# A transformer layer on one core: the next batch's input transposed in 64-row halves

## The reference

```python
x = L0_attn_x                                   # (8, 512, 256)
x = x + attn(layernorm(x), gamma, w_qkv, w_out)
x = x + ffn(layernorm(x), router_w, w1, b1, w2, b2)

# attn: xn = x / max(norm(x), 1e-12) * 16 * (gamma + 1)
#       q, k, v = split(xn @ w_qkv)             # 16 heads of 64
#       out = softmax(q * 64**-0.5 @ k.T) @ v @ w_out
# ffn:  p = top-2 of softmax(x @ router_w), divided by its sum
#       out = (gelu(x @ w1 + b1) @ w2 + b2) * sum(p)
```

## Time and profile before

| | |
|---|---|
| median of 3 runs | 1197.71 us (1197.66 to 1198.62) |
| profiled execution | 1198.14 us, its span 1196.3 us |
| TensorE busy | 1183.7 us (99%) |
| VectorE busy | 961.9 us (80%) |
| ScalarE busy | 884.3 us (74%) |
| GpSimd busy | 640.1 us (54%) |
| eight transpositions of an input (L610) | 1.04 us |

### The profile page before, as it was taken

How to read it: one execution, slowest core, us unless ns; L and a number is a source line. 1 busy time by engine, 2 the same in 40 slices (tenths; PEclk the granted TensorE clock), 3 DMA queues, 4 the chain that set the end, 5 groups by cost and what they waited for, 6 DMA issues and landing times. The chain is left out here.

```text
span 1196.3 us, 29198 instructions
## 1 busy us (share of the span) xinstructions
PE 1183.7 (99%) x11347; PEld 1040.4 (87%) x11347; DVE 961.9 (80%) x1714; ACT 884.3 (74%) x1914; POOL 640.1 (54%) x809
## 2 busy tenths in 40 slices
PE   8999999999999999999999999999999999999999
PEld 6778888888888888888888888888888888988988
DVE  7788789878988888888888888889888987666644
ACT  6888788888887888788888887888888884334432
POOL 5776556555655565556555655555555674222221
PEclk9999999999999999999999999999999999999999
DMA  4222111311121113111311131113111232121100
GB/s 132 66 77 66 34 40 30 95 25 35 36 88 35 37 37 89 37 37 37 89 37 36 37 89 37 36 37 89 37 37 37 72 86 79 36 69 39 36 19 36
DMA packets 35240, 62.91 MB, mean 53 GB/s; under 512 B 5920, under 2 KB 12576, under 8 KB 35104
## 3 DMA queue, kind: packets, MB, share of 16 engines
q1 hardware_dynamic: 35104, 61.05, 19.0%
HBM read 19.08 MB, written 8.39 MB: 23 GB/s over the span
## 5 line engine op out<-in xcount | busy, mean ns | idle before, releaser
L927 POOL TENSOR_SCALAR prob<-prob,rowinv 128x512 f32<-128x512 f32 x512 | 350.2, 699 | 290.6 <-DVE rowinv L1116 290.2
L836 ACT ACTIVATE prob<-ps,negmax 128x512 f32<-128x512 f32 x512 | 347.0, 686 | 34.1 <-DVE negmax L1111 29.7
L1035 DVE TENSOR_TENSOR pT_lo<-ps,pT_hi 128x512 fp32r<-128x512 f32 (+1 forms) x384 | 320.4, 862 | 26.0 <-ACT pT_hi L829 21.3
L1111 DVE TENSOR_REDUCE negmax<-ps 128x2 f32<-128x1024 f32 x256 | 311.1, 1215 | 1.3 <-PE ps L524 1.2
L826 ACT ACTIVATE pT_hi<-ps 128x1024 fp32r<-128x1024 f32 x128 | 131.7, 1029 | 99.3 <-issue 98.7
L552 PEld LDWEIGHTS ps<-identity,prob 64*128 64x128 f32 x4096 | 154.7, 138 | 57.9 <-issue 18.2
L552 PE MATMUL ps<-identity,prob 64*128 64x64 f32 x4096 | 177.1, 226 | 3.4 <-DVE vbuf L1035 2.6
L518 PE MATMUL ps<-nat 64*128 64x512 f32 x1024 | 172.1, 413 | 1.5 <-ACT prob L836 0.5
L566 PE MATMUL ps<-pT_hi,vbuf 128*128 128x256 f32 x1024 | 164.8, 283 | 1.7 <-DVE pT_lo L1035 1.6
L566 PE MATMUL ps<-pT_lo,vbuf 128*128 128x256 f32 x1024 | 164.5, 283 | 0.0
L829 ACT ACTIVATE pT_hi<-ps 128x512 fp32r<-128x512 f32 x256 | 140.4, 610 | 16.5 <-PE ps L552 16.5
(11 more groups left out here) (119 smaller groups left out, 2307.1 us busy)
## 6 DMA issues: line engine op xcount, KB each, us to landing
att_hi_v<-halves_out SPq DMA_DIRECT2D x128, 128.0 KB, 2.3
att_lo_v<-halves_out SPq DMA_DIRECT2D x128, 128.0 KB, 2.3
xres<-in_x SPq DMA_DIRECT2D x8, 512.0 KB, 3.4
x_scratch<-xres SPq DMA_DIRECT2D x8, 512.0 KB, 3.1
out_y<-f_o SPq DMA_DIRECT2D x15, 256.0 KB, 2.0
xin<-in_x SPq DMA_DIRECT2D x7, 512.0 KB, 3.8
wstage<-in_w SPq DMA_DIRECT2D x4, 512.0 KB, 3.6
wstage<-in_w_qkv SPq DMA_DIRECT2D x6, 256.0 KB, 3.1
```

Source lines behind the costliest of these rows:

```text
L836: act.activation(prob[:, n % NPROB, j * SEQ:(j + 1) * SEQ], ps[:, PS_SCORE[n % 2] + j, :], ACT.Exp, bias=negmax[:, n % 4, j:j + 1], accum_ ...
L927: return pool.tensor_scalar(dst, src, scalar, 1.0, ALU.mult, ALU.mult)
L1035: return dve.tensor_tensor(dst, full, hi, ALU.subtract)
L1111: dve.tensor_reduce(negmax[:, n % 4, :], ps[:, PS_SCORE[n % 2]:PS_SCORE[n % 2] + 2, :], AX.X, ALU.max, negate=True).then_inc(s_max, 1)
```

## The change

The input's eight 128 by 128 transpositions become sixteen of 64 rows: half r = 0 is the first 64 rows of each 128-row tile and goes to bank 6, half r = 1 the others and goes to bank 7. Both groups of columns k lie in each bank. All sixteen are issued when the first of the two blocks comes up; the second block issues nothing but its waits. ScalarE rounds the half in bank 6, VectorE the half in bank 7, both in two instructions (one for each k, 256 elements to a partition, as each k has its own scale), and the remainders are four instructions in place of two. The output in `xT` is the same. Batch 0 stays as it was. The eighth input is now shared by the two engines in this way too, with a scale of 1.0.

```diff
         def split_by_vector(kind, *args):
-            return kind == "xt" and args[1] == KT - 1 and 1 <= args[0] < B
+            return kind == "xt" and args[1] == 1 and args[0] >= 1
+
+        def input_half(part, k, r):
+            return xT[part][:, k, :].rearrange("p (t r q) -> p t r q", t=TT, r=2)[:, :, r]
+
+        def input_in_psum(block_no, k):
+            return ps[:, aux_bank(block_no), k * TT * DH:(k + 1) * TT * DH].rearrange("p (t q) -> p t q", t=TT)
+
+        def input_scale(b, k):
+            return gain[:, k:k + 1] if b < B else 1.0
...
+            def transpose_input(bank):
+                for k in range(KT):
+                    for t in range(TT):
+                        for r in range(2):
+                            rows = slice(r * DH, (r + 1) * DH)
+                            column = (k * TT + t) * DH
+                            ins = pe.transpose(ps[:, bank + r, column:column + DH],
+                                               xn[rows, t, k * P:(k + 1) * P], identity[rows, rows])
+                            if k == KT - 1 and t == TT - 1:
+                                ins.then_inc(s_auxfull, 1)
...
+                    if b >= 1:
+                        if k == 0:
+                            transpose_input(aux_bank(block_no))
+                        return
...
                 if kind == "xt":
-                    b, k = args
+                    b, part = args
                     if b == 0:
                         act.wait_ge(s_gain, 1)
-                    scale = gain[:, k:k + 1] if b < B else 1.0
-                    ins = act.activation(xT[0][:, k, :], bank, ACT.Copy, scale=scale)
+                        ins = act.activation(xT[0][:, part, :], bank, ACT.Copy, scale=gain[:, part:part + 1])
+                    else:
+                        for k in range(KT):
+                            ins = act.activation(input_half(0, k, part), input_in_psum(block_no, k), ACT.Copy,
+                                                 scale=input_scale(b, k))
...
                 if kind == "xt":
...
+                        for k in range(KT):
+                            ins = lo(input_half(1, k, part), input_in_psum(block_no, k), input_half(0, k, part),
+                                     input_scale(b, k))
...
-            def input_hi(block_no, place, kind, b, k):
+            def input_hi(block_no, place, kind, b, part):
                 dve.wait_ge(s_auxfull, block_no + 1)
-                link(dve.tensor_scalar(xT[0][:, k, :], ps[:, aux_bank(block_no), :], gain[:, k:k + 1], None, ALU.mult))
+                for k in range(KT):
+                    ins = dve.tensor_scalar(input_half(0, k, part), input_in_psum(block_no, k), input_scale(b, k),
+                                            None, ALU.mult)
+                link(ins)
```

More of the change, by code:

```diff
@@ L606, in aux @@
                         pe.wait_ge(s_const, 16 * N_CONST)
+                    if b >= 1:
+                        if k == 0:
+                            transpose_input(aux_bank(block_no))
+                        return
                     for t in range(TT):
-                        if b == 0 and k == 0:
+                        if k == 0:
                             pe.wait_ge(s_xn_first, t + 1)
@@ L1057, in aux_done @@
                 if kind == "xt":
-                    k = args[1]
-                    scale = gain[:, k:k + 1] if args[0] < B else None
-                    ins = lo(xT[1][:, k, :], bank, xT[0][:, k, :], scale)
+                    b, part = args
+                    if b == 0:
+                        ins = lo(xT[1][:, part, :], bank, xT[0][:, part, :], gain[:, part:part + 1])
+                    else:
+                        for k in range(KT):
+                            ins = lo(input_half(1, k, part), input_in_psum(block_no, k), input_half(0, k, part),
+                                     input_scale(b, k))
                 elif kind == "q":
```

## The result

| | before | after |
|---|---|---|
| median of 9 runs, us | 1197.73 (1197.55 to 1198.62) | 1201.34 (1200.52 to 1202.55) |
| profiled execution, us | 1198.14 | 1201.29 |
| its span, us | 1196.3 | 1199.5 |
| granted TensorE clock | 1.0 | 1.0 |

The change made the kernel slower: ratio 1.003, 95% interval 1.002 to 1.004, which is +3.6 us on the medians and +3.15 on the two profiled executions. The forecast of 1199.3 us and its range, which ended at 1200.9, were both missed.

The account below looks back on a forecast made before the run. TensorE, 99% busy, was taken to be held at the changed places by VectorE's `vbuf`, then ScalarE's queue. 7 x 0.27 − 0.27 = +1.6 us gave 1199.3 us against the median, range 1196.9 to 1200.9.

Parts of the forecast that it names:

- TensorE's transpositions: Input transpositions end 0.24 us earlier per batch, worth nothing because the next TensorE instruction still waits for VectorE's `vbuf`.
- Rival D: Saved TensorE time arrives in full at all eight inputs: 3.1 us faster, 1194.6 us; chance 0.07.
- The wait: TensorE's idle time before the odd probability tile, released by `vbuf`, grows from 0.16 to about 0.40 us.
- ScalarE: At seven scaled inputs, ScalarE's exponential and with it TensorE's second score tile come 0.27 us later.
- Start: ScalarE begins rounding its half 0.14 us later, since that half is complete only with the fifteenth transposition.
- split: Two scaled 256-element ScalarE activations in place of one of 512 cost 0.13 us more per batch.
- place: Second score tile's delay at each of seven scaled inputs, +0.27 us, bounds 0 to +0.51.
- Rival C: Split activations and roundings are as cheap as plain ones: 0 per batch, −0.3 at the eighth, 1197.4 us; chance 0.16.
- VectorE: VectorE's remainders end 0.36 us later, query product 0.17 later, beside ScalarE's 0.27 and not on top.
- The eighth: At the eighth input, ScalarE takes two unscaled 256-element pieces, gaining 0.27 us; VectorE's extra work is hidden by idle time.
- used a step on: GpSimd's probabilities wait for VectorE's reciprocal, 0.36 us later, but are used a step on: costed at nothing.
- The sum: Seven scaled inputs at +0.27 us and −0.27 at the eighth give +1.6 us for the whole run.

Follow-up runs that it names:

- a2: Kernel after, with the second input block's waits on TensorE removed ahead of the odd probability tile; 1200.73 us, ratio 1.002 to the kernel before.
- a3: Kernel after, with ScalarE rounding its half in one unscaled activation of 512 elements in place of two of 256; 1200.96 us, ratio 1.0022 to the kernel before.
- a4: Kernel after, with VectorE's rounding and both remainders each one 512-element instruction, using one gain column; 1202.53 us, ratio 1.0031 to the kernel before.
- c1: Kernel before, with only the eighth input transposed in 64-row halves and the seven scaled ones as before; 1198.24 us, ratio 0.9998.
- b2: Kernel after, with 64 tiny matmuls in place of six warming ones at the start; 1201.62 us, ratio 1.0023 to the kernel before.
- c3: Kernel after, with 32 tiny matmuls in place of three warming ones at the start; 1200.88 us, ratio 1.0021 to the kernel before.
- b1: Kernel before, with 64 tiny matmuls in place of six warming ones at the start; 1199.45 us, ratio 1.0005.
- b3: Kernel before, with 128 tiny matmuls in place of ten warming ones at the start; 1202.47 us, ratio 1.0029.
- a1: Kernel after timed again with no edit, as the base for the others on this chip; 1201.67 us, ratio 1.0031 to the kernel before.
- c2: Kernel after, with the eighth input in the old form and only the seven scaled inputs changed; 1200.87 us, ratio 1.0022 to the kernel before.
- c4: Kernel after, with ScalarE's second exponential ahead of its input rounding at seven places, VectorE's order matched; 1201.56 us, ratio 1.0027 to the kernel before.
- b4: Kernel before, with ScalarE's second exponential ahead of the input's rounding at the seven scaled places, VectorE's order matched; 1198.95 us, ratio 1.0001.

## Why the prediction was wrong

*TensorE's transpositions are worth nothing: right.* The group takes 0.71 us, it starts 0.21 behind the last L576 start of its kind (0.09 for the shape, as forecast), and the wait behind it grew. Rival D's 3.1 us never came. The pairs are 1.5 times as fast as the full ones (1.04 for 0.71 us), not nearly twice as the prediction has it there. The wait was to grow to 0.40 and is 0.53, because five piled waits release L562 0.16 later than `vbuf` alone did; a2 shows that this costs nothing.

*ScalarE: right.* Start +0.15 (forecast +0.14), split +0.16 (forecast +0.13), place +0.29 (forecast +0.27). a3 removes the split, and the second score tile follows. Rival C, splits as cheap as plain ones, is out. The estimate by the Trainium skill (VectorE: DVE Perf Modes, its section on the TRN2 errata) was +0.14 for the split; the runs show 0.16, a little nearer to it than to the extrapolated 0.13.

*VectorE: right.* +0.36 to its end, as forecast, and not the gate (a4). With ScalarE's split gone (a3) it holds the query product at +0.17, the number that the prediction gave for VectorE alone.

*The eighth: the step that failed in part.* Its −0.27 appeared as −0.28. But the sum took it as kept, and cost GpSimd at nothing ("used a step on"). In the kernel after, 0.38 is given back in steps 126 and 127, by GpSimd's late probabilities. The reason is not the 0.36 us that the prediction had priced at nothing, since c1, b2 and c3 have that too and keep the gain. It is an attention half whose issue on SyncE took 0.8 us longer, so that it landed 0.8 us later.

*The sum: the step that failed.* "7 x 0.27 − 0.27 = +1.6 us" added up places and counted everything between and behind them as unchanged: nothing for what happens behind the eighth place and in the feed-forward half, where +0.38 and +0.49 were measured. The prediction spoke of SyncE's queue nowhere. It also took the 64 added TensorE instructions by their time alone. They move the instruction packets against the rest of the program. In the kernel after one falls on the issues at the eighth place, and one on the `x1` store. Of the 1.5 us that the profile has above the forecast (3.15 for 1.6), 0.15 are the terms at the places, 0.4 the give-back at the eighth, 0.5 the feed-forward half, 0.3 strays and 0.2 the start. The last two are scatter. The medians lie another 0.45 us further apart than the two profiled executions, and no trace shows that part.

What is shown and what is not. That the added instructions move packets is shown (b1 to b3, c3). That a packet on the eighth's issues takes the gain back is shown by c3 and b2 against a1 and after, and by c2 from the other side; b1 shows that the price can be nothing. In c4 the packet comes at 973.5, behind the issues but among their transfers; the half lands after 4.2 us for 3.2 in the kernel after, GpSimd waits 2.08, and 1.25 is lost.

The store lasts 4.4 to 5.2 us in five of the six unfilled kernels in which all eight inputs are changed, and in these the packet starts 1.1 to 2.15 us behind the store's issue. In c2, b1 and a2 it starts 2.2 to 2.5 us behind it, and the store takes 2.6 to 3.1. The long store costs TensorE 0.4 to 1 us in four kernels, by way of VectorE and ScalarE. b2 and c3 keep the work, move the packet off the store and lose nothing there; c4 shows that this price too can be nothing. The other loss of the feed-forward half, 0.20 to 0.35 us, is TensorE waiting for VectorE's additions. b1 and b3 have it too, with the old form throughout, so it does not come from the change's own instructions; why VectorE is late there stays open.

Open too are short gaps of 0.2 to 0.3 us, most of them inside TensorE's transposition groups, that come at other steps in each trace (their sum differs by −0.7 to +0.7 us), and a2's 0.9 us. The first weighted values also start 0.1 to 0.7 us later in the profiles of unfilled kernels with no edit near the start, which is scatter. That is why the last microsecond cannot be divided further with single profiles.

No version ran faster than the kernel before: c1 and b4 are level with it.

## What to carry to other kernels

Where TensorE waits just behind the work you shorten, look for what stands in the queue of the engine it next waits for: a change that saves TensorE 0.3 us and puts 0.3 us ahead of a decisive exponential costs 0.3 us. Where two gates lie within 0.3 us of each other, lifting one of them yields half of what it promises (a3), or nothing when the other is pushed back for it (b4, c4). And a sum over the edited places is not the sum of the run: hold each stage of the new trace against the old, and when an unedited stage has moved, look at the DMA queues before the engines.

## What the runs showed of the hardware

- Instruction packets of 16 KB come on queue q8, beside the data's q1, in the profile's view of the 16 DMA engines. At the eighth place a SyncE issue of 0.60 us that meets one takes 1.19 to 1.89 us. In the fourteen traces 153 issues behind the first 100 us take over 1 us (1.03 to 2.21), and for each a packet starts between 0.26 us before the issue and 0.15 after it; where the packet starts 0.38 us or more into an issue of an attention half, that one stays at 0.66 or less, and the issue right behind it, if there is one, is the long one. The 512 KB store in the feed-forward half took 2.6 us alone, 4.4 to 5.2 with a packet 1.1 to 2.15 us behind its issue, and 2.6 to 3.1 with one 2.2 to 2.5 behind. From 1.49 MB for 2 × 11347 TensorE instructions I estimate 66 bytes each, if the packets are mostly TensorE's; 128 instructions more are then half a packet.
- A wait with no instruction behind it on its engine joins the next instruction's. With five waits L562 started 0.21 us after the last release, with the second block's removed 0.06.
- Scaled 256-element activations from PSUM start 0.36 us apart, scaled 512 ones 0.57; plain ones 0.27 and 0.49. VectorE's scaled 256 pieces run 0.39 apart.
- A change of tile shape on TensorE cost 0.09 us, from L495 to L552 as from L576 to L605 (0.21 from start to start for 0.12).
